# Weights times values of a cross attention, head by head in two column tiles of 64

## The chip, the cores and the metric

The kernel runs on one core of a Trainium2 chip. The metric is the time of one execution in microseconds (us), as the median of several runs; lower is better. The core's engines are TensorE (PE in the profile; its weight loads are listed apart as PEld), VectorE (DVE), ScalarE (ACT), GpSimd (POOL) and SyncE (SP), which issues the transfers here. They run side by side and are ordered by semaphores.

## What is computed

The reference is two layers, each with a cross attention, an attention and a feed-forward part, on x of 8 x 64 x 512. The change touches the cross attention of the second layer: 64 queries of each of 8 batches attend over 1601 context rows and one null key, with 16 heads of 64 features.

```python
q = _split_heads(jnp.einsum('bnd,df->bnf', x, Wq))
kv = jnp.einsum('bmc,cf->bmf', context, Wkv)
k, v = jnp.split(kv, 2, axis=-1)
k, v = (_split_heads(k), _split_heads(v))
...
k = jnp.concatenate((nk, k), axis=-2)
v = jnp.concatenate((nv, v), axis=-2)
q = q * scale
sim = jnp.einsum('bhid,bhjd->bhij', q, k)
attn = jax.nn.softmax(sim, axis=-1)
out = jnp.einsum('bhij,bhjd->bhid', attn, v)
...
out = jnp.einsum('bnf,fd->bnd', out, Wout)
```

The line that matters is the second product, `attn` with `v`, for each batch and head a sum over 1602 keys.

## The kernel before

The program is a row of stages. The first ones (depooling, a state-space layer, a quantised feed-forward layer, the queries) run with ValueWork beside them, which computes the values v of all batches ahead of time and writes them to `vd` in DRAM. Then comes attend(), the stage that the change touches (its tiles are named `ca_...`), then the output projection (`co_...`), a head attention (`ha_...`) and experts (`ex_...`).

attend() works on pairs of heads: NF = 64 pairs, f = 8 b + p for batch b and pair p. The 128 partitions of the scores hold both heads' 64 queries (first head 0 to 63, second head 64 to 127). Every operand that needs more than half precision is split into a high and a low f16 part, so each product is three matmuls: high with high, high with low, low with high.

For one pair, PE computes `ca_p_w` (project(), queries times key weights, 24 matmuls in two parts of 12), the scores `ca_p_s` in four pieces of columns (chunk(), 24 matmuls for each piece, on 448, 448, 353 and 352 keys) and one column for the null key (null_of(), three matmuls). ACT takes the exponentials, DVE and ACT write the weights as two f16 parts into `parts`, and SP's transposing DMAs turn them into `turned`: keys on the partitions, [key, part, key tile, 128], the last axis being first head's queries, then second head's. SP also loads the pair's values from `vd` into `vals`: [key, key tile, part, 128], the last axis being both heads' features. Both have two buffers, used by f % 2, and are filled again once `av_done` says that their product is done.

The product is attend_to(f), lines 1457 to 1471. For each of the JT = 13 key tiles of 128 keys (66 in the last, the null key included) it issues three matmuls (lines 1468 to 1470) with all 128 features of `vals` as the stationary operand and all 128 columns of `turned` as the moving one. The result in `p_o` is 128 features by 128 columns, four pairs beside one another in one bank. In it the first head's features with the first head's queries and the second's with the second's are wanted; the other two quarters are each head's values with the other's weights and aren't read. After four pairs, DVE's leave() (lines 1580 to 1589) copies the wanted quarters into `o_t` with one instruction for each head, on 64 partitions each, and `o_copied` lets PE go on.

The order on PE is written by hand (lines 1474 to 1489). In the loop over f, the product of pair f - 2 stands between the second and third piece of the scores of pair f, and the null key's three matmuls are the first of the third piece. The product's neighbours on PE are thus matmuls with 448 and with 1 moving column, and all of them use 128 stationary columns:

```python
if f < NF:
    chunk(f, 1)
if f >= 2:
    attend_to(f - 2)
if f < NF:
    chunk(f, 2)
```

Of the kernel before, what the change touches and what calls it, by code (L numbers as in the profile page):

```python
# [23 lines left out]
ALU = mybir.AluOpType  # L24
# [3 lines left out]
P = 128  # L28
B, S, D = 8, 64, 512
# [170 lines left out]
HEADS, DH = 16, 64  # L200
PAIRS = HEADS // 2
GROUPS = 2
GP = PAIRS // GROUPS
CC = CW // P
JT = (CTX + P - 1) // P
KEYS = CTX + 1
LAST = CTX - (JT - 1) * P
W_UP = 64.0
# [1007 lines left out]
P_UP = 4096.0  # L1216
# [67 lines left out]
def attend(nc, io, k, q_parts, o_t, vd, wkt, halves):  # L1284
# [10 lines left out]
    with Stage(nc, "ca") as st:  # L1295
# [4 lines left out]
        turned = [st.sb(f"turned{s}", [P, 2, JT, P], f16) for s in range(2)]  # L1300
        vals = [st.sb(f"vals{s}", [P, JT, 2, P], f16) for s in range(2)]
# [7 lines left out]
        p_o = st.ps("p_o")  # L1309
# [22 lines left out]
        def splits(f):  # L1332

            b, p = divmod(f, PAIRS)
            if b + 1 == B or p == 0:
                return []
            return [b * JT + p - 1] + (list(range(b * JT + EARLY, (b + 1) * JT)) if p == PAIRS - 1 else [])

        def tile_of(i):

            b, j = i // JT + 1, i % JT
            h = j >= EARLY
            at = j * P - h * HALF_KEYS
            return ctx[(2 * b + h) % 3], b, j, h, slice(at, at + tile_rows(j))

        @block.sync
        def _(sp):
            def load(i):
                if i >= LATER:
                    return  # L1350
                if i >= 3:
                    sp.wait_ge(ctx_low, i - 2)
                _, b, j, _, _ = tile_of(i)
                sp.dma_start(stage[i % 3][:, :], io.ctx_t[b, j, :, :]).then_inc(ld[i % 3], 16)

            def load_values(f):
                b, p = divmod(f, PAIRS)
                if f >= 2:
                    sp.wait_ge(av_done, f - 1)
                v = vals[f % 2]  # L1360
                sp.dma_start(v[:, 0:FULL, :, :].rearrange("p j l f -> p j (l f)"),
                             vd[b, p, 0:FULL * P, :, :].rearrange("(j k) l f -> k j (l f)", k=P)).then_inc(ld_v[f % 2], 16)
                sp.dma_start(v[0:LAST, FULL, :, :].rearrange("p l f -> p (l f)"),
                             vd[b, p, FULL * P:CTX, :, :].rearrange("k l f -> k (l f)")).then_inc(ld_v[f % 2], 16)

            def turn(f):
                if f == 0:
                    sp.wait_ge(pad_zero, 1)
                if f >= 2:
                    sp.wait_ge(av_done, f - 1)  # L1370
                for l in range(2):
                    sp.wait_ge(wl_done if l else wh_done, f + 1)
                    sp.dma_start(turned[f % 2][:, l, :, :], parts[:, l, :], transpose=True).then_inc(t_done[f % 2], 16)

            sp.dma_start(nk[:, :], io.null_k).then_inc(ld_null, 16)
            sp.dma_start(nv[:, :], io.null_v).then_inc(ld_null, 16)
            load_values(0)
            load_values(1)
            for i in range(3):
                load(i)  # L1380
            sp.wait_ge(null_low, 2)
            for s in range(2):
                sp.dma_start(vals[s][LAST:LAST + 1, FULL, :, :], nv_parts[:, :, :]).then_inc(null_set, 16)
            for f in range(NF + 1):
                if f:
                    turn(f - 1)
                if 2 <= f < NF:
                    load_values(f)
                if f < NF:
                    for i in splits(f):  # L1390
                        load(i + 3)
# [18 lines left out]
        @block.tensor  # L1410
        def _(pe):
            def project(f, r):

                pe.wait_ge(q_ready, 2 * f + 2)
                if 2 * f + r:
                    pe.wait_ge(qw_low, 2 * f + r)
                p, q = f % PAIRS, q_diag[f % 2]
                for i in range(CC // 2):
                    c = (r * CC // 2 + i) * P
                    o = p_w[:, i * P:(i + 1) * P]  # L1420
                    nc.tensor.matmul(o, wkt[0][:, p, c:c + P], q[:, 0, :], start=True, stop=False)
                    nc.tensor.matmul(o, wkt[0][:, p, c:c + P], q[:, 1, :], start=False, stop=False)
                    last = nc.tensor.matmul(o, wkt[1][:, p, c:c + P], q[:, 0, :], start=False, stop=True)  # L1423
                last.then_inc(qw_ready, 1)

            def chunk(f, n):
                b, h = f // PAIRS, n // 2
                if n % 2 == 0:
                    if 2 * f + h >= 3:
                        pe.wait_ge(exp_done, 2 * f + h - 2)  # L1430
                    if n == 0:
                        pe.wait_ge(qw_low, 2 * f + 2)
                    if b and f % PAIRS == 0:
                        pe.wait_ge(ctx_low, (b - 1) * JT + (JT if h else EARLY))
                if n == 2:
                    null_of(f)
                x = ctx[(2 * b + h) % 3]
                lo, hi = CUTS[n] - h * HALF_KEYS, min(CUTS[n + 1], CTX) - h * HALF_KEYS
                o = bank(f, n)[:, 0:hi - lo]
                a = qw[f % 2]  # L1440
                for c in range(CC):
                    nc.tensor.matmul(o, a[:, 0, c, :], x[:, 0, c, lo:hi], start=(c == 0), stop=False)  # L1442
                    nc.tensor.matmul(o, a[:, 0, c, :], x[:, 1, c, lo:hi], start=False, stop=False)  # L1443
                    last = nc.tensor.matmul(o, a[:, 1, c, :], x[:, 0, c, lo:hi], start=False, stop=(c == CC - 1))  # L1444
                if n % 2:
                    last.then_inc(half_done, 1)

            def null_of(f):
                if f == 0:
                    pe.wait_ge(null_low, 1)  # L1450
                at = CTX - CUTS[3]
                o, q = bank(f, 3)[:, at:at + 1], q_diag[f % 2]
                nc.tensor.matmul(o, q[:, 0, :], nk_parts[:, 0:1], start=True, stop=False)
                nc.tensor.matmul(o, q[:, 0, :], nk_parts[:, 1:2], start=False, stop=False)
                nc.tensor.matmul(o, q[:, 1, :], nk_parts[:, 0:1], start=False, stop=True)

            def attend_to(f):
                G, p = divmod(f, GP)
                if G and p == 0:
                    pe.wait_ge(o_copied, G)  # L1460
                if f == 0:
                    pe.wait_ge(null_set, 32)
                pe.wait_ge(ld_v[f % 2], 32 * (f // 2 + 1))
                pe.wait_ge(t_done[f % 2], 32 * (f // 2 + 1))
                o, v, a = p_o[:, p * P:(p + 1) * P], vals[f % 2], turned[f % 2]
                for j in range(JT):
                    w = tile_rows(j) + (j == JT - 1)
                    nc.tensor.matmul(o, v[0:w, j, 0, :], a[0:w, 0, j, :], start=(j == 0), stop=False)
                    nc.tensor.matmul(o, v[0:w, j, 0, :], a[0:w, 1, j, :], start=False, stop=False)
                    last = nc.tensor.matmul(o, v[0:w, j, 1, :], a[0:w, 0, j, :], start=False, stop=(j == JT - 1))  # L1470
                last.then_inc(av_done, 1)

            project(0, 0)
            project(0, 1)
            for f in range(NF + 2):
                if f < NF:
                    chunk(f, 0)
                if f + 1 < NF:
                    project(f + 1, 0)
# [6 lines that stand above are left out]
                if f + 1 < NF:  # L1486
                    project(f + 1, 1)
                if f < NF:
                    chunk(f, 3)
# [54 lines left out]
        def _(dve):  # L1544
# [34 lines left out]

            def leave(G):  # L1580
                b, g = divmod(G, GROUPS)
                dve.wait_ge(av_done, (G + 1) * GP)
                dve.wait_ge(q_ready, 2 * (G + 1) * GP)
                for h in range(2):
                    ins = nc.vector.tensor_scalar(
                        o_t[h * DH:(h + 1) * DH, b, g * GP:(g + 1) * GP, :],
                        p_o[h * DH:(h + 1) * DH, :].rearrange("p (c h s) -> p c h s", h=2, s=S)[:, :, h, :],
                        1.0 / (W_UP * P_UP), None, ALU.mult)
                ins.then_inc(o_copied, 1)

            dve.wait_ge(null_high, 2)
            nc.vector.scalar_tensor_tensor(nk_parts[:, 1:2], nk[:, :], W_UP, nk_parts[:, 0:1], ALU.mult,
# [1284 lines left out]
```

## Time and profile before

| | us |
|---|---|
| median of 3 runs | 3235.72 |
| lowest, highest | 3234.48, 3242.55 |
| the profiled execution | 3228.4 |
| its span | 3226.7 |
| PE busy in it | 2927.9 (91%) |
| DVE busy | 1506.7 (47%) |
| ACT busy | 1012.3 (31%) |
| stretch 1467 to 2709 (products of the cross attention) | 1242 |

The profile comes from one execution. Instructions are listed with the kernel's line, what they write and what they read. The duration of a matmul includes its way through the array, so that several overlap and the durations add up to more than the time; the distance between their starts tells how fast they follow each other. A form such as "128*128 128x448" gives the stationary operand (partitions * columns) and the moving one (partitions x columns).

### The profile page before, as it was taken

The page shows a single profiled execution, that of the slowest core. Times are in us where ns is not written, and L with a number is a line of the kernel's source. Part 1 is how long each engine was busy: PE and PEld are TensorE (multiplying, and loading weights), DVE is VectorE, ACT ScalarE, POOL GpSimd, SP SyncE. Part 2 cuts the span into 40 slices and gives each one's busy share as a digit, 9 for nine tenths or more (in the row PEclk, how much of TensorE's full clock was granted, in tenths as well). Part 3 has the DMA queues.
Part 4 walks back from the last instruction along what each step waited for, and adds up shares of the span by engine and source line. Part 5 has one row for each costly group of instructions (what it writes and reads, how often), then busy time and mean ns, then how long its engine had stood idle before and what let it go on. Part 6 is the DMA issues. An engine that isn't in the chain of part 4 may idle for free. (4 is left out here: it accounts for less than half of the span.)

```text
span 3226.7 us, 40186 instructions
## 1 busy us (share of the span) xinstructions
PE 2927.9 (91%) x17021; PEld 1616.3 (50%) x17029; DVE 1506.7 (47%) x1769; ACT 1012.3 (31%) x1525; POOL 68.6 (2%) x189
## 2 busy tenths in 40 slices
PE   6979999977989999989999999999999997636799
PEld 3324444433444444446666666666666664415453
DVE  5359999974633222333434343434343432376410
ACT  3344334313422221222323232323232321284210
POOL 1000000000000000000000000000000000010000
PEclk9989999988999999999999999999999998867999
DMA  5123343333323333444556554546464543102203
GB/s 198 59 73 92 93 145 89 92 101 140 96 91 121 102 99 103 129 116 110 142 115 143 114 143 110 143 114 143 112 143 110 117 84 85 53 20 46 95 10 143
DMA packets 472619, 341.52 MB, mean 106 GB/s; under 512 B 232212, under 2 KB 437333, under 8 KB 467832
## 3 DMA queue, kind: packets, MB, share of 16 engines
q1 hardware_dynamic: 472440, 338.95, 38.7%
q8 instruction: 135, 2.21, 0.3%
q14 instruction: 44, 0.36, 0.0%
HBM read 226.60 MB, written 54.62 MB: 87 GB/s over the span
## 5 line engine op out<-in xcount | busy, mean ns | idle before, releaser
L366 PE MATMUL vw_pv<-vw_wv,vw_ctx 128*128 128x512 f16 (+1 forms) x1296 | 496.8, 383 | 63.0 <-DVE vw_vst L386 27.6
L367 PE MATMUL vw_pv<-vw_wv,vw_ctx 128*128 128x512 f16 (+1 forms) x1296 | 496.4, 383 | 0.0
L368 PE MATMUL vw_pv<-vw_wv,vw_ctx 128*128 128x512 f16 (+1 forms) x1296 | 495.5, 382 | 0.0
L1442 PE MATMUL ca_p_s<-early_halves,ca_qw 128*128 128x448 f16 (+2 forms) x1408 | 466.7, 331 | 1.4 <-DVE ca_qw L1555 1.4
L1443 PE MATMUL ca_p_s<-early_halves,ca_qw 128*128 128x448 f16 (+2 forms) x1408 | 466.7, 331 | 0.0
L1444 PE MATMUL ca_p_s<-early_halves,ca_qw 128*128 128x448 f16 (+2 forms) x1408 | 466.6, 331 | 0.0
L1555 DVE TENSOR_TENSOR ca_qw<-ca_p_w,ca_qw 128x512 f16<-128x512 f32 x128 | 88.5, 691 | 545.6 <-ACT ca_qw L1505 545.6
L386 DVE TENSOR_TENSOR vw_vst<-vw_pv,vw_vst 128x512 f16<-128x512 f32 x162 | 110.8, 688 | 376.9 <-ACT vw_vst L377 376.8
L1505 ACT ACTIVATE ca_qw<-ca_p_w 128x512 f16<-128x512 f32 x128 | 76.4, 597 | 558.8 <-PE ca_p_w L1423 558.8
L377 ACT ACTIVATE vw_vst<-vw_pv 128x512 f16<-128x512 f32 x162 | 95.4, 593 | 468.4 <-PE vw_pv L368 468.4
L366 PEld LDWEIGHTS vw_pv<-vw_wv,vw_ctx 128*128 128x128 f16 (+1 forms) x1296 | 127.7, 99 | 228.9 <-issue 39.9
L1444 PE MATMUL ca_p_s<-ca_ctx,ca_qw 128*128 128x448 f16 (+2 forms) x640 | 215.4, 337 | 0.0
L1443 PE MATMUL ca_p_s<-ca_ctx,ca_qw 128*128 128x448 f16 (+2 forms) x640 | 215.4, 337 | 0.0
L1442 PE MATMUL ca_p_s<-ca_ctx,ca_qw 128*128 128x448 f16 (+2 forms) x640 | 215.4, 337 | 0.0
L368 PEld LDWEIGHTS vw_pv<-vw_wv,vw_ctx 128*128 128x128 f16 (+1 forms) x1296 | 127.8, 99 | 156.7 <-issue 6.2
L367 PEld LDWEIGHTS vw_pv<-vw_wv,vw_ctx 128*128 128x128 f16 (+1 forms) x1296 | 127.6, 98 | 154.2 <-issue 7.2
L1444 PEld LDWEIGHTS ca_p_s<-early_halves,ca_qw 128*128 128x128 f16 x1408 | 137.8, 98 | 99.1 <-issue 0.9
L1513 ACT ACTIVATE ca_probs<-ca_p_s,ca_small 128x896 f32<-128x896 f32 (+1 forms) x128 | 117.7, 925 | 220.3 <-DVE ca_small L1564 220.3
L1442 PEld LDWEIGHTS ca_p_s<-early_halves,ca_qw 128*128 128x128 f16 x1408 | 137.7, 98 | 90.5 <-DVE ca_qw L1555 1.7
L1443 PEld LDWEIGHTS ca_p_s<-early_halves,ca_qw 128*128 128x128 f16 x1408 | 137.8, 98 | 88.7 <-issue 0.7
L1577 DVE SCALAR_TENSOR_TENSOR ca_parts<-ca_probs,ca_small,ca_parts 128x1602 f16<-128x1602 f32 x64 | 120.9, 1889 | 119.0 <-ACT ca_parts L1522 119.0
L873 ACT ACTIVATE work<-early_halves,mb_a_neg 128x252 f32<-128x252 f32 x256 | 104.7, 491 | 218.1 <-DVE ms_h L905 215.5
(439 smaller groups left out, 4700.3 us busy)
## 6 DMA issues: line engine op xcount, KB each, us to landing
vw_ring<-in_ctx_t SPq DMA_DIRECT2D x109, 512.0 KB, 3.7
vd<-vw_vst SPq DMA_DIRECT2D x192, 256.0 KB, 2.3
ca_vals<-vd SPq DMA_DIRECT2D x64, 768.0 KB
ca_stage<-in_ctx_t SPq DMA_DIRECT2D x91, 512.0 KB, 3.6
ex_w_d<-in_w_d SPq DMA_DIRECT2D x8, 2048.0 KB, 7.1
early_r<-state_rows SPq DMA_DIRECT2D x8, 1024.0 KB, 8.1
early_r<-in_w SPq DMA_DIRECT2D x2, 4096.0 KB, 15.7
vw_ring<-in_w_kv SPq DMA_DIRECT2D x8, 512.0 KB, 4.7
```

The source lines that it names most:

```text
L366: self.nc.tensor.matmul(o, xh[:, c, 0:w], self.wv[0][:, c, f], start=(c == 0), stop=False)
L367: self.nc.tensor.matmul(o, xh[:, c, 0:w], self.wv[1][:, c, f], start=False, stop=False)
L368: last = self.nc.tensor.matmul(o, xl[:, c, 0:w], self.wv[0][:, c, f], start=False, stop=(c == CC - 1))
L377: self.nc.scalar.activation(self.staged(u, 0), self.bank(u).rearrange("p (c n) -> p c n", n=P), ACT.Copy).then_inc(self.vhi, 1)
L386: self.nc.vector.tensor_tensor(self.staged(u, 1), self.bank(u).rearrange("p (c n) -> p c n", n=P), self.staged(u, 0), ALU.subtract).then_i ...
L873: ins = nc.scalar.activation(da[q][:, m, :, 1:], steps, ACT.Exp, scale=a_neg[:, e, q * NQ + m:q * NQ + m + 1])
L1442: nc.tensor.matmul(o, a[:, 0, c, :], x[:, 0, c, lo:hi], start=(c == 0), stop=False)
L1443: nc.tensor.matmul(o, a[:, 0, c, :], x[:, 1, c, lo:hi], start=False, stop=False)
L1444: last = nc.tensor.matmul(o, a[:, 1, c, :], x[:, 0, c, lo:hi], start=False, stop=(c == CC - 1))
L1513: nc.scalar.activation(probs[:, CUTS[2 * h]:CUTS[2 * h + 2]].rearrange("p (a n) -> p a n", a=2), scores(f, h), ACT.Exp, bias=nbias, scale= ...
L1555: nc.vector.tensor_tensor(qw[f % 2][:, 1, c, :], p_w[:, :].rearrange("p (c n) -> p c n", n=P), qw[f % 2][:, 0, c, :], ALU.subtract).then_i ...
L1577: nc.vector.scalar_tensor_tensor(parts[:, 1, 0:KEYS], probs[:, :], rinv, parts[:, 0, 0:KEYS], ALU.mult, ALU.subtract).then_inc(wl_done, 1)
```

## The change

Each matmul of the product becomes two, one for each head: its 64 features (stationary) with its 64 queries' weights (moving), into its own 64 partitions of `p_o`. The matmuls alternate between the first and the second head within each of the three kinds. The unwanted quarters are no longer computed; `p_o` holds four pairs in 256 columns instead of 512. Both last matmuls of a pair count up `av_done`, so those who wait for it (SP twice, DVE once) wait for twice the number. leave() needs one instruction for both heads.

```diff
@@ load_values and turn (SP)
-                    sp.wait_ge(av_done, f - 1)
+                    sp.wait_ge(av_done, 2 * (f - 1))
@@ attend_to (PE)
-                o, v, a = p_o[:, p * P:(p + 1) * P], vals[f % 2], turned[f % 2]
+                v, a = vals[f % 2], turned[f % 2]
+                heads = [slice(h * DH, (h + 1) * DH) for h in range(2)]
+                o = [p_o[h, p * S:(p + 1) * S] for h in heads]
                 for j in range(JT):
                     w = tile_rows(j) + (j == JT - 1)
-                    nc.tensor.matmul(o, v[0:w, j, 0, :], a[0:w, 0, j, :], start=(j == 0), stop=False)
-                    nc.tensor.matmul(o, v[0:w, j, 0, :], a[0:w, 1, j, :], start=False, stop=False)
-                    last = nc.tensor.matmul(o, v[0:w, j, 1, :], a[0:w, 0, j, :], start=False, stop=(j == JT - 1))
-                last.then_inc(av_done, 1)
+                    for i, h in enumerate(heads):
+                        nc.tensor.matmul(o[i], v[0:w, j, 0, h], a[0:w, 0, j, h], start=(j == 0), stop=False)
+                    for i, h in enumerate(heads):
+                        nc.tensor.matmul(o[i], v[0:w, j, 0, h], a[0:w, 1, j, h], start=False, stop=False)
+                    for i, h in enumerate(heads):
+                        last = nc.tensor.matmul(o[i], v[0:w, j, 1, h], a[0:w, 0, j, h], start=False, stop=(j == JT - 1))
+                        if j == JT - 1:
+                            last.then_inc(av_done, 1)
@@ leave (DVE)
-                dve.wait_ge(av_done, (G + 1) * GP)
+                dve.wait_ge(av_done, 2 * (G + 1) * GP)
                 dve.wait_ge(q_ready, 2 * (G + 1) * GP)
-                for h in range(2):
-                    ins = nc.vector.tensor_scalar(
-                        o_t[h * DH:(h + 1) * DH, b, g * GP:(g + 1) * GP, :],
-                        p_o[h * DH:(h + 1) * DH, :].rearrange("p (c h s) -> p c h s", h=2, s=S)[:, :, h, :],
-                        1.0 / (W_UP * P_UP), None, ALU.mult)
-                ins.then_inc(o_copied, 1)
+                nc.vector.tensor_scalar(o_t[:, b, g * GP:(g + 1) * GP, :], p_o[:, 0:GP * S].rearrange("p (c s) -> p c s", s=S),
+                                        1.0 / (W_UP * P_UP), None, ALU.mult).then_inc(o_copied, 1)
```

No instruction changes its place: the product stands on PE where it stood, between the same neighbours. Its end on PE, with the null key's matmuls and the third piece of the scores behind it, reads before (`ca_turned` and `ca_vals` are what the product reads):

```order
5292 L1469 MATMUL ca_p_o<-ca_turned,ca_vals 128x128
5293 L1470 MATMUL ca_p_o<-ca_turned,ca_vals 128x128
5294 L1453 MATMUL ca_p_s<-ca_nk_parts,ca_q_diag 128x1
5295 L1454 MATMUL ca_p_s<-ca_nk_parts,ca_q_diag 128x1
5296 L1455 MATMUL ca_p_s<-ca_nk_parts,ca_q_diag 128x1
5297 L1442 MATMUL ca_p_s<-early_halves,ca_qw 128x353
```

And in the changed kernel, on the same place of PE, where "x2" stands for the two heads:

```order
5292 L1473 MATMUL ca_p_o<-ca_turned,ca_vals 64x64 x2
5293 L1475 MATMUL ca_p_o<-ca_turned,ca_vals 64x64 x2
5294 L1453 MATMUL ca_p_s<-ca_nk_parts,ca_q_diag 128x1
5295 L1454 MATMUL ca_p_s<-ca_nk_parts,ca_q_diag 128x1
5296 L1455 MATMUL ca_p_s<-ca_nk_parts,ca_q_diag 128x1
5297 L1442 MATMUL ca_p_s<-early_halves,ca_qw 128x353
```

Each row of the product has become two of 64 by 64, and its neighbours are the same.

## Rows read from the trace of the kernel before

**Rows 1.** The page's head: span, and busy time of each engine (share, instructions)

```profile
span 3226.7 us, 40186 instructions
...
PE 2927.9 (91%) x17021; PEld 1616.3 (50%) x17029; DVE 1506.7 (47%) x1769; ACT 1012.3 (31%) x1525; POOL 68.6 (2%) x189
```

**Rows 2.** Busy time of each engine in stretches (columns as in the head line)

```profile
core 0: us, PE busy (x) PEld busy (x) DVE busy (x) ACT busy (x) POOL busy (x), PEclk, DMA share, GB/s
1467.00:2709.00 1242.00, 1229.70 (x10045) 804.79 (x10042) 469.96 (x614) 377.63 (x522) 41.65 (x120) 1.00 0.53 122
```

**Rows 3.** PE's waits from 1467 to 2709 us: waiting line, releaser, total, times, longest

```profile
PE ca_p_o L1468 <- DMA ca_turned<-ca_parts: 9.3, 1, 9.3
PE ca_p_s L1453 <- ACT ca_probs L1513: 3.0, 6, 0.8
```

**Rows 4.** Instructions on ca_p_o: count, ns min/median/max, first and last start, forms

```profile
L1468 PE MATMUL ca_p_o<-ca_turned,ca_vals x832: 219/219/311, 1468.0 to 2708.7; 128*128 128x128 f16 x154, 66*128 66x128 f16 x13
...
L1585 DVE TENSOR_SCALAR work<-ca_p_o x32: 416/422/428, 1530.0 to 2709.5; 64x256 f32<-64x256 f32 x32
```

**Rows 5.** Timeline of PE around one product: start us, us, instruction

```profile
2002.12 0.35 PE L1442 MATMUL ca_p_s<-early_halves,ca_qw 128*128 128x448 f16 x1
...
2006.65 0.22 PE L1468 MATMUL ca_p_o<-ca_turned,ca_vals 128*128 128x128 f16 x1
2006.71 0.22 PE L1469 MATMUL ca_p_o<-ca_turned,ca_vals 128*128 128x128 f16 x1
...
2008.66 0.22 PE L1468 MATMUL ca_p_o<-ca_turned,ca_vals 66*128 66x128 f16 x1
...
2008.84 0.17 PE L1453 MATMUL ca_p_s<-ca_nk_parts,ca_q_diag 128*128 128x1 f16 x1
...
2008.92 0.31 PE L1442 MATMUL ca_p_s<-early_halves,ca_qw 128*128 128x353 f16 x1
```

**Rows 6.** Timeline of PE's weight loads at the product's start

```profile
2006.47 0.10 PEld L1468 LDWEIGHTS ca_p_o<-ca_turned,ca_vals 128*128 128x128 f16 x1
2006.66 0.10 PEld L1469 LDWEIGHTS ca_p_o<-ca_turned,ca_vals 128*128 128x128 f16 x1
```

**Rows 7.** Weight loads by shape: count, busy us, mean ns, idle before them

```profile
L1470 PEld LDWEIGHTS ca_p_o<-ca_turned,ca_vals 128*128 128x128 f16 x768 | 75.6, 98 | 0.0
...
L967 PEld LDWEIGHTS mo_p_out<-early_r,early_halves 128*128 128x128 f32 x64 | 12.2, 190 | 15.0 <-issue 14.8
...
L728 PEld LDWEIGHTS mi_p_dbc<-early_halves,mi_w_x 128*64 128x64 f32 x16 | 2.1, 137 | 4.8 <-issue 4.6 <-ACT early_halves L755 0.3
...
L368 PEld LDWEIGHTS vw_pv<-vw_wv,vw_ctx 128*8 128x8 f16 x16 | 1.4, 87 | 2.1
```

**Rows 8.** The position sums: timeline row, and its instructions by line (as rows 4)

```profile
3091.81 0.81 PE L2602 MATMUL ex_p_a<-ex_mask,ones 128*128 128x24 f32 x6
...
L2602 PE MATMUL ex_p_a<-ex_mask,ones x6: 256/263/269, 3091.8 to 3092.4; 128*128 128x24 f32 x2, 128*128 128x16 f32 x2, 128*128 128x8 f32 x2
```

**Rows 9.** Timeline of PE where the stationary columns change: three places

```profile
1398.54 0.38 PE L368 MATMUL vw_pv<-vw_wv,vw_ctx 128*128 128x512 f16 x1
1398.85 0.38 PE L366 MATMUL vw_pv<-vw_wv,vw_ctx 128*8 128x512 f16 x1
1399.07 0.38 PE L367 MATMUL vw_pv<-vw_wv,vw_ctx 128*8 128x512 f16 x1
...
142.75 1.02 PE L722 MATMUL mi_proj<-work,early_r 128*128 128x512 f32 x2
143.71 7.08 PE L728 MATMUL mi_p_dbc<-early_halves,mi_w_x 128*64 128x512 f32 x16
...
2778.07 0.60 PE L1897 MATMUL ha_ps<-ha_sqn,ha_pick 128*16 128x256 f32 x2
...
2778.61 1.09 PE L1879 MATMUL ha_ps<-ident,work 128*128 128x128 f32 x8
```

**Rows 10.** Timeline at the end of the stage

```profile
2708.79 0.22 PE L1470 MATMUL ca_p_o<-ca_turned,ca_vals 66*128 66x128 f16 x1
2709.04 0.86 DVE L1585 TENSOR_SCALAR work<-ca_p_o 64x256 f32<-64x256 f32 x2 [7.98 <-PE ca_p_o L1470]
...
2710.81 2.50 DVE L1657 COPY co_heads<-work 128x1024 f32<-128x1024 f32 x4 [0.91 <-PEq L73]
```

More of the change, by code:

```diff
@@ L1369, in turn @@
                 if f >= 2:
-                    sp.wait_ge(av_done, f - 1)
+                    sp.wait_ge(av_done, 2 * (f - 1))
                 for l in range(2):
```

## The prediction

> **What bounds the kernel now.** I read the page's head first, for the size of the whole, then the stretches, for the stage that the change touches. The profiled execution took 3228.4 us with a span of 3226.7 us, and TensorE (PE) is busy for 91% of it [rows 1]. The cross attention after its first products lies between 1467 and 2709 us: there PE is busy 1229.70 of 1242.00 us, while VectorE (DVE) has 470 and ScalarE 378, and the granted clock is 1.00, the higher level, 2.4 GHz [rows 2]. The list of PE's waits says the same: 9.3 us once, at the very end of the stage, and 3.0 us in six short ones [rows 3]. So in this stage each us that PE works longer or shorter is a us of the kernel. A "busy" matmul overlaps the next, so I price by the distance between starts in the timeline, not by the durations.
>
> **The product as it is.** It is 39 matmuls for each of 64 head pairs, 2496 in all (832 at each of three lines [rows 4]), each 128 columns of stationary values and 128 columns of weights. In the timeline they start 0.0557 us apart: from 2006.71 to 2008.66 are 35 steps [rows 5]. 2496 x 0.0557 is 139 us, 4.3% of the kernel. That is all that the change can shorten. The weight loads are hidden: one is listed 0.10 long, yet each starts with the matmul ahead of its own (the first at 2006.47 for the matmul at 2006.65, the next at 2006.66 for 2006.71) [rows 5, 6]. Half of each result (one head's weights with the other head's values) is never read.
>
> **Term 1, the matmuls themselves.** Each matmul becomes two of 64 x 64, one a head, so 4992 matmuls and as many loads. What counts is the time of a pair of halves against 0.0557 us. No row shows a matmul with 64 moving columns, so I bound it. Scores with 448 columns start 0.1888 apart (2002.12 to 2006.65 is 24 steps) and the product's with 128 columns 0.0557 [rows 5]: 0.000416 us a column, with 0.0025 left for each matmul. At 64 columns that is 0.0557 - 64 x 0.000416 = 0.0291 us. If the halves run one after the other, a pair is 0.0582 us, 0.0025 more than before: 2496 x 0.0025 = +6.2 us. The smallest step in the trace is that of the null key's matmuls, one column each: three steps from 2008.84 to 2008.92, so 0.027 us, with a load of 128 columns in each step [rows 5]. A pair paced at that is 0.054 us: 2496 x -0.0017 = -4.2 us. If the halves run side by side in the array, a pair takes 0.0291 us: 2496 x -0.0266 = -66.4 us. That is the lower end. The upper end comes from the loads. A load of 128 f16 columns takes 98 ns and one of 8 takes 87; f32 loads take 190 ns at 128 columns and 137 at 64, so 0.83 ns a column over a fixed 84 [rows 7]. The 8 f16 columns lie 3 ns over that 84, 0.4 ns a column: 64 would be 27 ns, just under the 29 of the matmul that hides it. If it were f32's pace, 53 ns a load and 0.107 a pair, each of the two loads of a pair would stand out. That f32 pace sets the step is seen in the position sums of the last stage: six of 128 f32 columns take 0.81 us, 0.26 of it the length of the last, so 0.11 apart though they move only 8 to 24 columns [rows 8]. That end is 2496 x (0.107 - 0.0557) = +128 us. I take +6.2: the rows of f16 in this stage are the nearest, and nothing in this trace shows two matmuls running side by side.
>
> The Trainium skill (TensorE: Matmul & The Clock Gate, section "Part 3: Packing small matmuls") says that matmuls in different column groups run concurrently, starting some 4 ns apart, and reports 2.38 times the speed for three tiles with 512 columns. By it a pair would be about 0.033 us (an estimate from that page), and the kernel would gain; no run here has such neighbours, and the result that it gives is rival 1.
>
> **Term 2, changing the array's shape.** The halves need another tile of the array than the scores before and the null matmuls behind. Where the trace goes to fewer stationary columns and back, a gap appears. From 128 to 8 columns (f16, 512 moving): starts at 1398.54 and 1398.85, 0.31 instead of the 0.22 that the next step takes, so 0.09 to 0.10 lost; and the load, elsewhere one matmul ahead, isn't ahead there. From 128 to 64 (f32): two matmuls of 0.59 span 1.02, so the second starts at 143.18, the 64-column one at 143.71: 0.53 instead of 0.43, 0.10 lost. From 16 back to 128: the second of two (0.60 long in all, step 0.21) starts near 2778.28, the next shape at 2778.61: 0.33 instead of 0.21, 0.11 lost [rows 9]. Each product is entered once and left once, but the last two follow each other: 63 entries and 63 exits, 126 x 0.105 = +13.2 us. Bounds: 0.09 gives +11; 0.2 each, if short halves hide less of the refill, gives +25; zero, if a 64-column tile were no change of shape, is spoken against by the second place.
>
> **Term 3, the copy out.** leave() becomes one instruction with 128 partitions instead of two with 64, of 422 ns each [rows 4]. Sixteen times 0.42 us of DVE are saved beside PE's work, in a stage where DVE is busy 38% of the time; what stands behind it there is the row maximum. Only the last copy is on the path: it waits for PE's last product, and the next stage begins behind it: -0.4 us [rows 10]. The doubled counts of av_done cost nothing. SP's transfers of values and turned weights wait for the product's end and would be issued up to 0.1 us later for 0.1 us more of product; they are used a pair and more later, over 19 us (1242 us over 64 pairs). Their cover would be gone only if PE's stage shrank by far more than any end above.
>
> **Sum.** +6.2 + 13.2 - 0.4 = +19.0 us. Against the profiled execution that is 3228.4 + 19.0 = 3247.4; the median of the runs shown, 3235.7, lies 7.3 higher, and the same sum on it gives 3254.7, which I forecast as 3255.
>
> **Rival 1, side by side (faster).** The halves use different columns of the array, different PSUM partitions and their own loads. If the array starts the second head's matmul while the first one's columns still stream, a pair takes 0.0291 and the sum is -66.4 + 13.2 - 0.4 = -53.6: 3182. It needs both heads' loads to run side by side too, since two of 27 ns in a row are already 54. Speaking for it: the loads run on beside the matmuls now. Against: only one load is ever ahead [rows 6], and four instructions in 0.029 us is twice the rate of any row, the null matmuls' two in 0.027. It wins from a pair of 0.0506 down, where term 1 pays for term 2.
>
> **Rival 2, paced by the instruction (no change).** The 0.027 of the null matmuls is the pace at which load and matmul are taken, whatever their width, and side by side or not a pair is 0.054. Then -4.2 + 13.2 - 0.4 = +8.6: 3244. It differs from the forecast only by how much of the 64 columns shows.
>
> **Rival 3, the loads stand out (much slower).** If narrow loads run at the f32 pace, a pair is 0.107: +128 + 13.2 - 0.4 = +141, 3377. For it: the fast f16 load is seen only with all 128 columns, and 84 + 14 ns for 128 columns but 84 + 3 for 8 means that full loads have a way four times as fast a column. Against: the 8-column row's 0.4 ns a column. It is the bound as soon as a load takes more than 29 ns.
>
> The Trainium skill (TensorEngine Tiling (Array Packing), section "Restrictions") says that column tiling turns the fast weight load off, and in the Trainium skill (TensorE: Matmul & The Clock Gate, section "LDWEIGHTS (loading the stationary operand)") a load takes its columns divided by 1.2 GHz. That would be 53 ns for 64 columns, an estimate from those pages equal to rival 3's; the 8-column row speaks for half of it.
>
> **How the numbers follow.** Forecast, one after the other: 43%. Side by side: 27%. Instruction pace: 12%. Loads stand out: 18%. About 0.3% (9.7 us) is what a measurement of this kernel can tell from no change. Faster 0.27 (rival 1); same 0.15 (rival 2, and a forecast with smaller gaps); slower 0.58. The range goes from rival 1, 3180, to the forecast with gaps of 0.2 us and some 0.004 us more a pair, 3278; rival 3 is left out with its 18%. The forecast's own range is 3244 to 3278.
>
> **What would show it.** In the timeline of the new product: starts every 0.029 us for the forecast, 0.027 for rival 2, two close together and then a pause of some 0.03 for rival 1, 0.053 for rival 3. A product that takes 2.19 us now should take 39 x 0.058 = 2.27 plus a gap of about 0.1 at either side. The listed load should be near 110 ns; near 137 means rival 3. The forecast is wrong if the pair's step is not near 0.058, or if the gaps at the change of shape are missing.

## The result, and the profile after

The changed kernel takes 3202.4 us (median of 4 runs, 3195.2 to 3207.5) against 3238.0 for the kernel before, a ratio of 0.989 (95% interval 0.9872 to 0.9907): 35.6 us faster. The forecast was 3255, slower by 0.6%. It went as rival 1 said, the two heads side by side, but with two thirds of its gain.

The head of the page after, to be read beside [rows 1]: 4984 instructions more (2496 matmuls and as many loads were added and 16 DVE instructions dropped; a few matmul records are missing from the trace before), and PE still bounds the kernel.

```profile
span 3193.4 us, 45170 instructions
...
PE 2885.4 (90%) x19525; PEld 1556.0 (49%) x19525; DVE 1498.5 (47%) x1753; ACT 1012.0 (32%) x1525; POOL 68.5 (2%) x189
```

The stretches answer [rows 2]. The stage now ends near 2674 us, 35 earlier, with PE busy 1185.6 of 1207 us; behind it everything takes as long as before (519.4 us; 517.7 then), at a granted clock of 0.85.

```profile
core 0: us, PE busy (x) PEld busy (x) DVE busy (x) ACT busy (x) POOL busy (x), PEclk, DMA share, GB/s
1467.00:2674.00 1207.00, 1185.61 (x12542) 744.73 (x12542) 462.21 (x599) 378.44 (x522) 41.63 (x120) 0.99 0.58 126
2674.00:3193.40 519.40, 376.73 (x1189) 210.22 (x1184) 197.96 (x366) 160.20 (x269) 14.17 (x23) 0.85 0.18 62
```

One product in PE's timeline, beside [rows 5]. "x2" stands for two matmuls of one line, the two heads.

```profile
2009.54 0.35 PE L1444 MATMUL ca_p_s<-early_halves,ca_qw 128*128 128x448 f16 x1
2009.82 0.22 PE L1471 MATMUL ca_p_o<-ca_turned,ca_vals 128*64 128x64 f16 x2
2009.87 0.20 PE L1473 MATMUL ca_p_o<-ca_turned,ca_vals 128*64 128x64 f16 x2
...
2011.04 0.20 PE L1475 MATMUL ca_p_o<-ca_turned,ca_vals 66*64 66x64 f16 x2
2011.17 0.18 PE L1453 MATMUL ca_p_s<-ca_nk_parts,ca_q_diag 128*128 128x1 f16 x1
```

The lines come every 0.03 us, each with both heads: from 2009.87 to 2011.04 are 37 steps, 0.0316 us for a pair. Side by side in one array, 78 matmuls take 1.23 us where 39 took 2.13. At either side stands the gap of the changed shape: 0.28 instead of 0.19 between the last 448-column matmul and the first half, 0.13 instead of 0.06 at the exit. The loads, beside [rows 6] and [rows 7]:

```profile
2009.35 0.10 PEld L1444 LDWEIGHTS ca_p_s<-early_halves,ca_qw 128*128 128x128 f16 x1
2009.82 0.11 PEld L1471 LDWEIGHTS ca_p_o<-ca_turned,ca_vals 128*64 128x64 f16 x2 [0.37 <-issue]
2009.84 0.11 PEld L1473 LDWEIGHTS ca_p_o<-ca_turned,ca_vals 128*64 128x64 f16 x2
```

Two loads start together for each line and carry on at the same 0.03 us. The first pair isn't ahead of its matmul (its start is 2009.82, the matmul's too, and the load before it stands at 2009.35): that is the entry gap. The instructions on ca_p_o, beside [rows 4], show the narrow load at 113 ns, near the 110 that its columns were worked out to, and the copy out as 16 of 424 ns:

```profile
L1471 PEld LDWEIGHTS ca_p_o<-ca_turned,ca_vals x1664: 106/113/157, 1469.1 to 2673.9; 128*64 128x64 f16 x171, 66*64 66x64 f16 x14
...
L1590 DVE TENSOR_SCALAR work<-ca_p_o x16: 424/424/425, 1528.0 to 2674.4; 128x256 f32<-128x256 f32 x16
```

PE's waits in the stage, beside [rows 3]:

```profile
PE ca_p_s L1453 <- ACT ca_probs L1519: 11.3, 7, 2.7
PE ca_p_o L1471 <- DMA ca_turned<-ca_parts: 10.1, 1, 10.1
```

The wait for the exponentials has grown from 3.0 to 11.3 us. This is where a part of the gain went.

**The account.** Starts of matmuls, summed over the stage from its first to its last, give 1293.7 us before and 1258.0 after, a difference of 35.6:

| | us |
|---|---|
| 64 products, from first to last start 1.227 instead of 2.125 us | -57.5 |
| entries, 0.283 instead of 0.189 us from the last score matmul | +5.8 |
| exits, 0.128 instead of 0.055 us to the null key's | +4.5 |
| late exponentials: seven of these exits are 11.8 us longer in all than the others, instead of 4.2 | +7.6 |
| the 353-column matmuls behind two of those waits, at half the clock | +3.0 |
| wait of the last product, 10.1 instead of 9.3 | +0.8 |
| together | -35.8 |

The exits' row counts the gaps between starts; the list of waits above has 8.3 us for the same thing. The 0.2 us too many are small changes of both signs in the null key's own matmuls and in the last product.

**Where the waits stand.** They come once per batch, at the null key's matmuls, the first of the third piece of the scores. At the longest one the timeline of ScalarE reads:

```profile
2344.25 0.60 ACT L1511 ACTIVATE ca_qw<-ca_p_w 128x512 f16<-128x512 f32 x1 [6.96 <-PE ca_p_w L1423]
2344.75 2.94 ACT L1505 ACTIVATE early_halves<-ca_stage 128x1024 f16<-128x1024 f32 x3
2352.07 1.06 ACT L1505 ACTIVATE early_halves<-ca_stage 128x1024 f16<-128x1024 f32 x1 [4.38 <-DMA ca_stage<-in_ctx_t]
...
2358.05 0.65 ACT L1505 ACTIVATE early_halves<-ca_stage 128x520 f16<-128x520 f32 x1 [2.44 <-DMA ca_stage<-in_ctx_t]
2360.52 1.01 ACT L1519 ACTIVATE ca_probs<-ca_p_s,ca_small 128x896 f32<-128x896 f32 x1 [1.82 <-DVE ca_small L1570]
```

and that of VectorE:

```profile
2358.73 0.71 DVE L1554 TENSOR_TENSOR early_halves<-ca_stage,early_halves 128x520 f16<-128x520 f32 x1 [1.86 <-ACT early_halves L1505]
2359.35 0.89 DVE L1566 TENSOR_REDUCE ca_small<-ca_p_s 128x1 f32<-128x706 f32 x1
```

At a batch's end the second halves of the next context are split, seven tiles instead of one. ScalarE idles 6.96 us for the projected queries before it may start them, idles again 4.38 us for a stage buffer to be loaded, and ends the last split at 2358.7. VectorE has the row maximum behind its own splits (2359.35), so the exponentials begin at 2360.52, and PE:

```profile
2361.67 0.19 PE L1453 MATMUL ca_p_s<-ca_nk_parts,ca_q_diag 128*128 128x1 f16 x1 [2.75 <-ACT ca_probs L1519]
...
2362.02 0.50 PE L1443 MATMUL ca_p_s<-early_halves,ca_qw 128*128 128x353 f16 x1
2362.32 0.50 PE L1444 MATMUL ca_p_s<-early_halves,ca_qw 128*128 128x353 f16 x1
```

After 2.75 idle us the scores' steps are 0.30 instead of 0.15 us, at a granted clock of 0.50 between 2362 and 2364 us: the clock has fallen from 2.4 to 1.2 GHz, and the wait costs another 1.3 us. The same befell the next batch's wait (1.6 us more). The other five, shorter ones left the clock at 1.00.

### The profile page after: what moved, and what is told of

The parts are those of the page before. It is cut to its first block and busy times, and to the rows that moved or that the text cites. A ratio compares the mean times of both kernels' runs of the same rounds, so it can differ in the third digit from the quotient of the medians.

```text
span 3193.4 us, 45170 instructions
## 1 busy us (share of the span) xinstructions
PE 2885.4 (90%) x19525; PEld 1556.0 (49%) x19525; DVE 1498.5 (47%) x1753; ACT 1012.0 (32%) x1525; POOL 68.5 (2%) x189
```

## The experiments

Each is the changed kernel with one edit unless another is named. "Product" is the time from the first to the last start of one pair's product. Ratios are to the kernel before, run on the same chip.

**The heads one after the other.** The same 78 matmuls, the first head's 39 first:

```diff
-for j in range(JT):
-    for i, h in enumerate(heads): ...
+for i, h in enumerate(heads):
+    for j in range(JT): ...
```

> The changed kernel, but with the 39 matmuls of the first head in a row and then the 39 of the second: the same 78 matmuls of 64 x 64, the same shapes, loads, copy and semaphores; only the order of the two heads is another. Theory (the gain comes from neighbours in different column tiles, which run side by side): each matmul now follows one of its own tile, so steps near 0.029 us, a product of 78 x 0.029 = 2.27 us instead of 1.23, and 64 x 1.04 = 67 us more than the changed kernel, less some 8 us of waits that go away: about 3260, slower than before by 15 to 25. Rival (two 64-column matmuls are cheap in any order, because half the array's work is left out or the step has no floor): within 10 us of the changed kernel, near 3202.

3261.0 us, ratio 1.008 (1.0063 to 1.0096): slower than before, and 58.6 us slower than the changed kernel, though nothing but the order differs. In PE's timeline:

```profile
2019.03 0.22 PE L1471 MATMUL ca_p_o<-ca_turned,ca_vals 128*64 128x64 f16 x1
2019.08 0.20 PE L1472 MATMUL ca_p_o<-ca_turned,ca_vals 128*64 128x64 f16 x1
...
2021.51 0.18 PE L1453 MATMUL ca_p_s<-ca_nk_parts,ca_q_diag 128*128 128x1 f16 x1
```

Steps of 0.032 us a matmul, as long as a pair took side by side, and a product of 2.36 us. The gain comes from the order, not from the narrow matmul; that it is the two column tiles is what the next run shows. This is also the kernel that my forecast described, within 6 us.

**The same order, but one column tile.** Both heads of a pair go into the same half of the partitions:

```diff
-o = [p_o[h, p * S:(p + 1) * S] for h in heads]
+o = [p_o[heads[p % 2], (p // 2 * 2 + i) * S:(p // 2 * 2 + i + 1) * S] for i in range(2)]
```

> The changed kernel with the matmuls in exactly its order, heads alternating, but both heads of a pair go into the same half of the partitions (lower half for even pairs, upper for odd ones), so both use the same column tile. The output is not the reference's, since half of the results land where the copy takes them for another head's. Theory: no two neighbours in different tiles, so the step is near 0.029 and the product 2.27 us, as with the heads apart; time near 3260. Rival (the alternation between two stationary operands is what makes it fast): two steps of 4 and 28 ns as in the changed kernel, near 3202.

The start flag is set for the first head's first matmul alone, and the stop flag for the second head's last.

One run: 3266.6 us, a product of 2.46 us.

```profile
2000.99 0.25 PE L1471 MATMUL ca_p_o<-ca_turned,ca_vals 128*64 128x64 f16 x2
2001.07 0.23 PE L1473 MATMUL ca_p_o<-ca_turned,ca_vals 128*64 128x64 f16 x2
...
2003.57 0.18 PE L1453 MATMUL ca_p_s<-ca_nk_parts,ca_q_diag 128*128 128x1 f16 x1
```

The "x2" lines are now 0.06 us apart instead of 0.03: the two matmuls of a line follow each other. Order, shapes and operands are those of the changed kernel; only where the result goes (and the two flags) has changed, and the whole gain is gone. The product is even 0.1 us longer than with the heads apart, where a few matmuls still run side by side (see the last experiment).

**As much saved without column tiles.** The kernel before, with one of the product's three kinds of matmuls left out:

```diff
-nc.tensor.matmul(o, v[0:w, j, 0, :], a[0:w, 1, j, :], start=False, stop=False)
```

> The kernel before, 128 x 128 matmuls and all, but with one of the product's three kinds left out (weights' low part with values' high part), 26 matmuls instead of 39: this shortens the product by 13 x 0.0557 = 0.72 us, as much as the change does by itself (2.37 to 1.64 us from the last score matmul before to the null key's first behind), without any change of the array's shape. The result lacks that term. Theory (of the 46 us that the products save, 8 to 11 come back as waits for the exponentials once per batch): the time falls by about 36, ratio 0.989, PE's waits for exponentials 10 to 12 us. Rival (the missing 11 us are a cost of the column tiles on their neighbours): the time falls by 44 to 47, ratio 0.986, waits near 3 us.

3199.6 us, ratio 0.9886 (0.9868 to 0.9904). From the last score matmul to the null key's first it takes 1.64 us, as in the changed kernel; and much the same comes back as waits:

```profile
PE ca_p_s L1453 <- ACT ca_probs L1512: 10.0, 7, 2.2
```

So the lost part isn't a cost of the tiles. Two kernels that shorten this stretch by 0.73 us, one with column tiles and one without, get some 36 us for their 47.

**Maximum and exponentials ahead of the last splits.**

```diff
 exps(f - 1, 0)
 exps(f - 1, 1)
+for i in splits(f - 1)[4:]: split_high(i)
...
-for i in splits(f): split_high(i)
+for i in splits(f)[:4]: split_high(i)
```

and the same for VectorE, behind offset().

> The changed kernel; at a batch's end ScalarE and VectorE split seven context tiles before they take up the last pair's row maximum and exponentials; here they split four, then take the maximum and exponentials, and split the other three behind them. Theory (the waits of 1.4 to 2.9 us once per batch are for the exponentials queued behind those splits, which themselves wait for DMAs): the wait for exponentials falls from 11.3 us to under 3, though some 0 to 4 us may come back as a wait for the splits; 5 to 8 us faster than the changed kernel, 3195. Rival (the splits' DMAs are what is late whatever the order): the wait only changes its name, within 2 us of 3202.

3199.4 us, ratio 0.9888 (0.9874 to 0.9903), 3 us less than the changed kernel in the medians and not told apart from it. The rival was nearer: most of the wait has changed its name.

```profile
PE ca_p_s L1454 <- DVE early_halves L1557: 7.0, 5, 2.4
PE ca_p_s L1454 <- DVE ca_ctx L1557: 2.4, 2, 1.2
```

PE now waits for the splits themselves, 9.4 us. What is late is the row of seven splits, not the exponentials behind it.

**Three splits earlier.** They no longer stand behind the projected queries of the next pair:

```diff
 weights_high(f - 1)
+for i in splits(f)[:3]: split_high(i)
 query_high(f + 1, 1)
-for i in splits(f): split_high(i)
+for i in splits(f)[3:]: split_high(i)
```

and so for VectorE around query_low(f + 1, 1).

> The changed kernel; of the context splits of a pair, ScalarE and VectorE do the first three (those whose tiles are loaded already) before they wait for the second half of the next pair's projected queries, not behind it. In the trace of the changed kernel ScalarE idles 7 us there once per batch, and the seven splits start only after that. Theory (PE's wait once per batch is for the last of seven splits and what is queued behind it, whose loads need slots that the first splits free): the splits start up to 5 us earlier, PE's waits in front of the third piece of scores fall from 11.3 us to under 3, and the kernel takes 3191 to 3196, 7 to 10 us less than the changed one. Rival (transposing and value DMAs on SyncE ahead of the context loads hold them back, so an earlier split frees slots that nobody refills): waits stay above 8 us, within 3 us of 3202.

3185.3 us, ratio 0.9834 (0.9812 to 0.9856), clear of the changed kernel's interval and 17 us below its median; the theory had 7 to 10. ScalarE at the same batch's end as above:

```profile
2332.17 1.04 ACT L1505 ACTIVATE early_halves<-ca_stage 128x1024 f16<-128x1024 f32 x1
2333.48 2.00 ACT L1505 ACTIVATE early_halves<-ca_stage 128x1024 f16<-128x1024 f32 x2 [0.27 <-PE ca_p_s L1444]
2339.23 0.60 ACT L1511 ACTIVATE ca_qw<-ca_p_w 128x512 f16<-128x512 f32 x1 [3.74 <-PE ca_p_w L1423]
2344.22 1.06 ACT L1505 ACTIVATE early_halves<-ca_stage 128x1024 f16<-128x1024 f32 x1 [4.39 <-DMA ca_stage<-in_ctx_t]
...
2350.14 0.65 ACT L1505 ACTIVATE early_halves<-ca_stage 128x520 f16<-128x520 f32 x1 [1.36 <-DMA ca_stage<-in_ctx_t]
```

The first three splits now fill the idle time before 2339.23, where the queries' copy starts. From that copy to the end of the last split (2350.14 and 0.65) it is 11.6 us; in the changed kernel it was 14.4 (2344.25 to 2358.7). PE's waits have nearly gone:

```profile
PE ca_p_s L1453 <- ACT ca_probs L1519: 2.2, 3, 1.4
```

The waits fell by 9 us; the stage from first to last matmul took 1245.5 us, 12.5 less, the 3.0 us of the lower clock with it. Of the 17 us between the medians the traces show 12.5 in the stage; the rest is within the scatter of the runs.

**A fourth stage buffer as well.** `stage` and its semaphores with four entries, four splits ahead.

> As the run before, with a fourth staging slot for context tiles and four splits ahead instead of three. Theory: one more tile is loaded ahead and one less waits for its DMA; waits of PE at the batch ends near 0 if the earlier splits alone left some; otherwise the same time as with three, within 3 us. Rival (SyncE's queue is what is late): the fourth slot brings what the earlier splits did not, 4 to 8 us.

3188.7 us, ratio 0.9842 (0.9818 to 0.9866), not to be told from three. No wait for exponentials or splits is left, and the stage is 1243.1 us, 2.4 less. Its profiled execution is nevertheless 6.8 us longer, all of it behind the stage, where the code is the same. First the stretch behind the stage with three buffers, then with four:

```profile
2663.00:3181.10 518.10, 375.89 (x1182) 209.82 (x1177) 197.98 (x366) 160.19 (x269) 14.17 (x23) 0.85 0.18 62
```

```profile
2658.00:3187.90 529.90, 387.42 (x1194) 217.49 (x1189) 198.18 (x366) 160.19 (x269) 14.17 (x23) 0.82 0.18 61
```

The stretch is 11.8 us longer, with a granted clock of 0.82 instead of 0.85 and PE busy 11.5 us more for the same work. A kernel's runs scatter by 3 to 13 us, and those of the changed kernel in the same sense: 3195.2 us at a mean clock of 0.955, 3207.5 at 0.951.

**The early splits in the kernel before.** The same edit on 128 x 128 matmuls.

> The kernel before, with 128 x 128 matmuls, and with the three context splits ahead of the second half of the projected queries, as in the run that put them ahead in the changed kernel. Theory (the early splits pay for the waits at the batch ends, and those were only 3.0 us in the kernel before and grew to 11.3 by the shorter product): 3 to 5 us less than before, ratio 0.9985, waits of PE for exponentials near 0; the 17 us that the changed kernel gained by them are mostly the change's own gain given free. Rival (the early splits are worth 15 us by themselves): ratio near 0.995.

3231.1 us, ratio 0.9975 (0.9964 to 0.9986). Its waits for exponentials are gone and the stage is 1289.6 us, 4.1 less. The early splits are worth 4 us in the kernel before and 12.5 in the changed one. With them the column tiles bring 1289.6 - 1245.5 = 44.1 us in the stage, not 35.6.

**How wide.** Each half takes all 128 columns of weights, and its result is 128 columns wide:

```diff
-nc.tensor.matmul(o[i], v[0:w, j, 0, h], a[0:w, 0, j, h], ...)
+nc.tensor.matmul(o[i], v[0:w, j, 0, h], a[0:w, 0, j, :], ...)
```

> The changed kernel, but each 64-column stationary operand takes all 128 moving columns (both heads' weights), so that as many products are computed as in the kernel before, in 4992 matmuls of 64 x 128 instead of 2496 of 128 x 128. The copy out takes the first 256 columns as before, so the output is not the reference's. Theory (two column tiles each work at the full array's pace side by side): two heads' matmuls in 0.053 to 0.062 us, a product of 39 x 0.058 = 2.3 us, about 64 x 1.05 = 67 us over the changed kernel less waits, 3258. Rival (side by side is only a matter of short matmuls hiding each other's start; streaming itself is shared): 2 x 0.053 for two heads, a product of 4.3 us, some 190 us over: 3390.

One run: 3251.1 us.

```profile
2014.42 0.25 PE L1471 MATMUL ca_p_o<-ca_turned,ca_vals 128*64 128x128 f16 x2
2014.50 0.22 PE L1473 MATMUL ca_p_o<-ca_turned,ca_vals 128*64 128x128 f16 x2
...
2016.57 0.22 PE L1475 MATMUL ca_p_o<-ca_turned,ca_vals 66*64 66x128 f16 x2
```

Two matmuls of 64 x 128 in 0.056 us, the product 2.15: the pace of one of 128 x 128. Two tiles stream fully beside each other, but with as many products as before nothing is gained: what the change saves is the unread half's moving columns, 0.0557 to 0.0316 us, a little less than half.

**How near the neighbours must be.** The heads alternate every 3, 6 or 18 matmuls:

```diff
-for i, h in enumerate(heads): (one matmul of each kind in turn)
+for i, h in enumerate(heads): (3, or those of two or of six key tiles)
```

> The changed kernel with the heads alternating every three matmuls (three of the first head, three of the second) instead of every one. Theory (a matmul starts 3 to 4 ns behind its neighbour if that is in the other tile, and some 30 ns behind it if in the same, strictly in program order): six matmuls take two steps of 4 and four of 30, 0.127 us, against 0.094 alternating and 0.184 with the heads apart; a product of 1.65 us and 64 x 0.42 = 27 us over the changed kernel less the waits of 8: 3221 to 3229. Rival (the queue lets a tile's matmul pass those of the other tile that stand ahead of it): 1.23 us as when alternating, 3202.

> The changed kernel with the heads alternating every six matmuls. In threes they took 1.234 us for a product, no more than one by one (1.227), so the other tile's matmuls pass those ahead of them. Theory (the queue looks some distance ahead; six matmuls with their loads are twelve instructions, within it): still 1.23 to 1.35 us for a product. Rival (it reaches only over about six instructions): 1.6 us or more, since part of each block then runs alone.

> The changed kernel with the heads alternating every eighteen matmuls (six key tiles a block, the last block three). With all 39 in a row the product took 2.36 us. Theory (the look ahead is limited to a few dozen instructions; eighteen matmuls with loads are 36): a product between 1.25 and 1.9 us. Rival (already at eighteen nothing overlaps): 2.3 us.

One run each for 3, 6 and 18; the other two rows are the medians from above. The times are of several chips; the products compare better:

| alternating every | product, us | time, us |
|---|---|---|
| 1 | 1.227 | 3202.4 |
| 3 | 1.234 | 3205.2 |
| 6 | 1.315 | 3210.1 |
| 18 | 2.064 | 3244.9 |
| 39 (heads apart) | 2.359 | 3261.0 |

My theory for threes, strict order, was wrong, and its rival right. In their timeline each line still has two matmuls that start together:

```profile
2013.09 0.23 PE L1471 MATMUL ca_p_o<-ca_turned,ca_vals 128*64 128x64 f16 x2
2013.14 0.21 PE L1472 MATMUL ca_p_o<-ca_turned,ca_vals 128*64 128x64 f16 x2
2013.17 0.21 PE L1473 MATMUL ca_p_o<-ca_turned,ca_vals 128*64 128x64 f16 x2
```

though the program has L1471, L1472, L1473 of the first head and then those of the second. A matmul doesn't wait for those of the other tile that stand ahead of it, as long as these are few. How few, the other three orders tell alike. In blocks of 6 the first three matmuls of a product run alone, and the second head's first starts beside the third, with three of the first head's six still to come:

```profile
2014.74 0.22 PE L1472 MATMUL ca_p_o<-ca_turned,ca_vals 128*64 128x64 f16 x1
...
2014.83 0.20 PE L1474 MATMUL ca_p_o<-ca_turned,ca_vals 128*64 128x64 f16 x1
2014.83 0.22 PE L1472 MATMUL ca_p_o<-ca_turned,ca_vals 128*64 128x64 f16 x2
```

In blocks of 18 fifteen run alone, from 2012.10 us on; the second head's first starts beside the fifteenth, again with three to come, and when these are done the second head is alone ("x1") until its own last three:

```profile
2012.57 0.20 PE L1474 MATMUL ca_p_o<-ca_turned,ca_vals 128*64 128x64 f16 x1
2012.57 0.22 PE L1472 MATMUL ca_p_o<-ca_turned,ca_vals 128*64 128x64 f16 x2
...
2012.69 0.20 PE L1472 MATMUL ca_p_o<-ca_turned,ca_vals 128*64 128x64 f16 x1
```

And with the heads apart it is the 36th of 39 (2020.15, 35 steps of 0.032 us behind 2019.03):

```profile
2020.15 0.20 PE L1473 MATMUL ca_p_o<-ca_turned,ca_vals 128*64 128x64 f16 x1
2020.16 0.22 PE L1471 MATMUL ca_p_o<-ca_turned,ca_vals 128*64 128x64 f16 x2
...
2020.28 0.20 PE L1471 MATMUL ca_p_o<-ca_turned,ca_vals 128*64 128x64 f16 x1
```

It is so in all 62 products of each run that stand between scores. So a matmul of the other tile is taken up when at most three unstarted ones (with their loads) stand ahead of it. In blocks of 3 there are never more, and of 6 only the first three and the last three of a product are alone: 1.227 + 3 x 0.03 = 1.32 us, and 1.315 was measured.

## Why the prediction was wrong

**What bounds the kernel:** right as to the engine: the time fell by 35.6 us, and so did the stage of PE. But "each us that PE works longer or shorter is a us of the kernel" held for 36 of 47 us only (see rival 1's sum).

**Term 1:** wrong, and this decides the sign. I took the halves to run one after the other, 0.0582 us a pair and +6.2 us; they run side by side, 0.0316 us, -57.5. The serial price itself was fair: the heads apart took 0.0613 a pair on the average, and their stage grew by 27.0 us where the sum had 19.0. What failed is the choice: "nothing in this trace shows two matmuls running side by side". That was no evidence against, since no place of the kernel before has two neighbours in different tiles, so no row could have shown it. The upper and lower end were bounded rightly by rows, and the only statement on the case itself came from the Trainium skill (TensorE: Matmul & The Clock Gate, section "Part 3: Packing small matmuls"), concurrent matmuls some 4 ns apart; the trace after agrees, with pairs of 3 to 4 ns between starts, and its estimate of 0.033 us was the nearest of all. I gave it 27%. The range holds 3202.4 only because it reaches down to rival 1; the forecast's own range, from 3244, doesn't.

**The arguments against rival 1:** both fell. That "only one load is ever ahead" holds for each tile, not for the array: two loads start together. "Four instructions in 0.029 us" is nearly what happens, in 0.0316; the 0.027 of the null key's matmuls is then not the pace at which instructions are taken, and rival 2 falls with it.

**The narrow load:** right. It is listed at 113 ns, 110 expected, and nothing like 53 ns is seen in the steps; rival 3 didn't come about. Whether the 2.5 ns by which the step of 0.0316 exceeds the 0.0291 worked out belong to the load or to the matmul, no run separates. The Trainium skill's rule that column tiling turns the fast load off (TensorEngine Tiling (Array Packing), section "Restrictions") fits the trace, 113 ns against 98 for twice the columns. Its columns over 1.2 GHz (TensorE: Matmul & The Clock Gate, section "LDWEIGHTS (loading the stationary operand)"), 53 ns here, doesn't: with the heads apart the steps are 0.032.

**Term 2:** right in kind, somewhat large: 0.094 at an entry and 0.073 at an exit instead of 0.105 each, 10.3 us instead of 13.2. The heads apart and both heads in one tile have the same gaps (0.282 and 0.128 us), so they belong to the shape and not to the two heads.

**Term 3:** right: 16 copies of 424 ns, off the path but for the last.

**Rival 1's sum** was -53.6; -35.6 came. The products brought 57.5 us where term 1 had 66.4, 9 us less (6 of them because a pair takes 0.0316 and not 0.0291 us); the gaps give 3 back. The rest, some 12 us, is the second step that failed: I listed the six short waits of [rows 3] but did not ask what they would grow to when PE's stage shrinks by 50 us. They stand where ScalarE and VectorE split seven context tiles in a row, which takes a fixed time, and PE comes there earlier. That this and not the tiles costs it is shown twice: by the kernel before with fewer matmuls (same time within 3 us, waits of 10.0 and 11.3 us), and by the early splits, which give it back. Where the product stays long the waits stay short, tiles or not: 3.5 us with the heads apart, 4.8 with 128 moving columns.

What stays open: why the reach over the other tile's matmuls is three, and why some waits are followed by the lower clock and others not. The runs give both, not their reason.

## What to carry to other kernels

If half of a product on 128 partitions is thrown away because two heads share them, compute each head's 64 columns into its own half of the partitions, and alternate the two so that neighbours use different column tiles; the wrong order turns the same instructions from 1.1% faster to 0.8% slower. Each change of the array's shape costs about 0.1 us on either side, so a row of narrow matmuls must be long enough to pay for 0.17 us. If strict alternation is awkward, blocks of three cost nothing (1.234 us) and blocks of six little (1.315). When PE is the bound and gets shorter, look at its shortest waits first: here moving three splits into ScalarE's idle time brought 12.5 us more in the stage, and the two together run at 0.983 of the kernel before.

## What the hardware showed that I had not expected

Matmuls on different column tiles start 3 to 4 ns apart when they alternate, and each tile keeps its own pace of 0.03 us for 64 columns, 0.056 for 128, loads included. They also overlap when up to three matmuls of one tile that haven't started stand ahead of the other tile's; in longer blocks only the last three run beside the other tile. And a wait of 2.75 us in a stage that is otherwise full was followed by some 3 us at 1.2 GHz, so it cost half as much again. That isn't sure to follow: with blocks of 6 a wait of 2.57 us left the clock at 1.00, and with blocks of 18 one of 1.7 us was followed by the lower one.
